# TensorE streams products of zeros between the small products of the landmark reading

## The chip, the cores and the metric

The kernel runs on one core of a Trainium2 chip. A core has TensorE (PE: products, its results go to the eight banks of PSUM), VectorE (DVE), ScalarE (ACT), GpSimd (POOL) and SyncE (SP), which here issues the DMAs. Each engine works through its own list of instructions in order and waits for the others on semaphores. The metric is the device time of one execution in microseconds (us), as the median of several runs; lower is better.

## The reference

A tower of one layer: a state-space tokenizer gives `h` of shape (16, 256, 512); an attention layer with landmarks and a feed-forward layer with block-wise quantized operands follow. The change lies in one step of the attention. There are 16 batch elements of 256 tokens, each cut in 4 blocks of 64 tokens (`S = 64`), with 4 landmarks per block (`M = 4`), 32 heads of 16 dimensions. After the landmarks have attended to one another, each reads the 64 tokens of its own block again:

```python
l2q = _split_heads(lmf @ w_l2t_q + b_l2t_q).reshape(B, H, Nb, M, DH)
ra = jax.nn.softmax(jnp.einsum('bhnmd,bhnsd->bhnms', l2q, kb) * scale, axis=-1)
ro = jnp.einsum('bhnms,bhnsd->bhnmd', ra, vb)
ro = ro.transpose(0, 2, 3, 1, 4).reshape(B, NL, D)
```

`kb` and `vb` are the rotated keys and the values of the tokens, computed in an earlier stage. All of it is float32.

## The kernel before

`build` runs seven stages, one after the other, each in its own `phase`: tokenizer, `attention_local`, `landmark_attention`, `landmarks_from_tokens`, `landmark_keys`, `attention_global`, `ffn`. At the end of a phase all engines meet at a barrier. Nothing of one stage runs beside another.

The change lies in `landmarks_from_tokens` alone. Its work is written out by hand for the 16 elements i, with two buffers of everything (`u = i % 2`). Per element:

- SP loads the keys `kT` and the values `v`, 512 KB each, from DRAM. The load of the keys of i waits until `scores(i-2)` is done, that of the values of i until `sums(i-2)` is done. SP issues in the order k(i), v(i), k(i+1), so the keys of i+1 also stand behind the wait of the values of i: they are issued right after `sums(i-2)`.
- DVE (`queries`) spreads the landmark queries over heads into `ql`.
- TensorE, `scores(i)` (L1490): 16 products, one for each block (Y = 4) and chunk of 128 channels (KC = 4), each with 32 stationary columns and 64 moving ones. The four chunks stand in four column groups of the array. A float32 product shows as two records in the profile, so there are 32.
- DVE, `maximum(i)` (L1441); ACT, `exp(i)` (L1405), 4 instructions with their sums; DVE, `norm(i)` (L1447, L1449).
- TensorE, `transposes(i)` (L1501): 2 transposes of 128x128.
- ACT, `copy(i)` (L1415): the transposed shares into `pT`.
- TensorE, `sums(i)` (L1513): 8 products with 128 stationary columns of `v` and 64 moving ones, 16 records.
- DVE, `pick(i)` (L1457, L1462): keeps each head's own part of the sums.

TensorE's order is: scores(0), and then for each i transposes(i), scores(i+1), sums(i). DVE's order is norm(i), queries(i+2), maximum(i+1), pick(i-1); ACT's is copy(i), exp(i+1). PSUM holds two banks each for scores, transposes and sums; two of its eight banks are unused in this stage.

Of the kernel before, what the change touches and what calls it, by code (L numbers as in the profile page):

```python
# [10 lines left out]
F32 = mybir.dt.float32  # L11
BF16 = mybir.dt.bfloat16
# [3 lines left out]
P = 128  # L16
# [1335 lines left out]
def landmarks_from_tokens(nc, K, k_s, v_s):  # L1352

    ctx = ExitStack()
    with ctx:
        def sb(name, shape, dt=F32):
            return ctx.enter_context(nc.sbuf_tensor("lt_" + name, shape, dt))

        def sem(name):
            return nc.alloc_semaphore("lt_" + name)  # L1360
# [4 lines left out]
        ql = sb("ql", [P, 2, KC, Y, 8 * M])  # L1365
# [1 line left out]
        pa = sb("pa", [P, 2, Y, S])  # L1367
        pT = sb("pT", [P, 2, 2, 2, P])
        lmx = sb("lmx", [P, KC * Y, M, 8])
        ps = ctx.enter_context(nc.psum_tensor("lt_ps", [P, 6, 512], F32))  # L1370
        scores_b = lambda u: ps[:, u]
        trans_b = lambda u: ps[:, 2 + u]
        sums_b = lambda u: ps[:, 4 + u]
        s_k, s_v = [[sem(f"{n}_in{u}") for u in range(2)] for n in ("k", "v")]
        s_zero, s_ql, s_sc, s_max, s_exp, s_rec, s_norm, s_tr, s_copy, s_sum, s_lmx, s_pick = (sem(n) for n in (
            "zero", "ql", "sc", "max", "exp", "rec", "norm", "tr", "copy", "sums", "lmxr", "pick"))
        block = ctx.enter_context(nc.Block())

        @block.sync
        def _(sp):  # L1380
            for i in range(BATCH):
                u = i % 2
                if i >= 2:
                    sp.wait_ge(s_sc, i - 1)
                sp.dma_start(kT[:, u].rearrange("p t c d -> p t (c d)"),
                             k_s[2 * i:2 * i + 2].rearrange("a p d -> p a d")).then_inc(s_k[u], 16)
                if i >= 2:
                    sp.wait_ge(s_sum, i - 1)
                sp.dma_start(v[:, u], v_s[2 * i:2 * i + 2].rearrange("a p d -> p a d")).then_inc(s_v[u], 16)

        @block.gpsimd
        def _(pool):
            pool.memset(pT[:], 0.0).then_inc(s_zero, 1)

        @block.scalar
# [83 lines left out]
        @block.tensor  # L1479
        def _(pe):  # L1480
            def scores(i):
                u = i % 2
                pe.wait_ge(s_k[u], 16 * (i // 2 + 1))
                pe.wait_ge(s_ql, i + 1)
                if i >= 2:
                    pe.wait_ge(s_exp, i - 1)
                for y in range(Y):
                    T, b = y // 2, y % 2
                    for k in range(KC):
                        ins = pe.matmul(scores_b(u)[32 * k:32 * k + 32, y * S:(y + 1) * S],  # L1490
                                        ql[:, u, k, y], kT[:, u, T, k, b * S:(b + 1) * S],
                                        start=True, stop=True)
                ins.then_inc(s_sc, 1)

            def transposes(i):
                u = i % 2
                pe.wait_ge(s_norm, i + 1)
                if i >= 2:
                    pe.wait_ge(s_copy, i - 1)
                for T in range(2):  # L1500
                    ins = pe.transpose(trans_b(u)[:, T * P:(T + 1) * P],  # L1501
                                       pa[:, u, 2 * T:2 * T + 2].rearrange("p b s -> p (b s)"), c("ident"))
                ins.then_inc(s_tr, 1)

            def sums(i):
                u = i % 2
                pe.wait_ge(s_v[u], 16 * (i // 2 + 1))
                pe.wait_ge(s_copy, i + 1)
                if i >= 2:
                    pe.wait_ge(s_lmx, i - 1)  # L1510
                for T in range(2):
                    for k in range(KC):
                        ins = pe.matmul(sums_b(u)[:, 128 * k + 64 * T:128 * k + 64 * T + 64],  # L1513
                                        v[:, u, T, k * P:(k + 1) * P], pT[:, u, T, :, 32 * k:32 * k + 32],
                                        start=True, stop=True)
                ins.then_inc(s_sum, 1)

            scores(0)
            for i in range(BATCH):
                transposes(i)  # L1520
                if i + 1 < BATCH:
                    scores(i + 1)
                sums(i)


# [686 lines left out]
class Kept:  # L2212
# [15 lines left out]
    def c(self, name):  # L2228
        a, b = CAT[name]
        return self.cst[:, a:b]  # L2230
# [24 lines left out]
def build(nc, A, consts_d, out):  # L2255
    def scratch(name, shape, dt=F32):
        return nc.dram_tensor(name, shape, dt, kind="Internal").ap()

    NT = 2 * BATCH
    h_s = scratch("h_s", (TOK, BATCH, D))  # L2260
    q_s, k_s, v_s = (scratch(n, (NT, P, D)) for n in ("q_s", "k_s", "v_s"))
    o_s = scratch("o_s", (NT, P, D + H))
    with ExitStack() as ctx:
        ctx.enter_context(nc.allow_non_contiguous_dma(reason="a few thousand scalars of parameters"))
        with phase(nc):
            tokenizer(nc, A, consts_d, h_s)
        K = Kept(nc, ctx)
        load_constants(nc, K, consts_d)
        with phase(nc):
            attention_local(nc, A, K, h_s, q_s, k_s, v_s, o_s)  # L2270
        with phase(nc):
            landmark_attention(nc, A, K, None)
        with phase(nc):
            landmarks_from_tokens(nc, K, k_s, v_s)
        gv_s = scratch("gv_s", (ROWS, D))
        with phase(nc):
            landmark_keys(nc, A, K, gv_s)
        h1_s = scratch("h1_s", (NT, P, D))
        with nc.sbuf_tensor("xqT", [P, KC, NT * P], BF16) as K.xqT:
            with phase(nc):  # L2280
                attention_global(nc, A, K, h_s, q_s, o_s, gv_s, h1_s)
            with phase(nc):
                ffn(nc, K, h1_s, out)
# [33 lines left out]
```

## Time and profile before

| | us |
|---|---|
| median of 3 runs | 1866.25 (1866.24 to 1870.73) |
| the profiled execution, its own time | 1858.75 |
| its span, first to last instruction | 1857.0 |
| PE busy | 1555.9 (84%) |
| DVE busy | 1378.5 (74%) |
| ACT busy | 986.5 (53%) |
| POOL busy | 495.0 (27%) |
| mean granted clock of TensorE | 0.872 |

The profile is one execution. A busy time of an engine is the union of its instructions' times. For TensorE that is no measure of how densely the array works: a product's record runs from its issue until its last result is out, so records of neighbours overlap, and small products that follow one another at twice their streaming time still make the engine 100% busy. PEclk is the clock that TensorE was granted, as a share of 2.4 GHz: 0.50 stands for 1.2 GHz. Mean durations of single records hold this tail; the distance from one product to the next is read from a run of equal ones: its length, less one record, over their number less one.

### The profile page before, as it was taken

What the parts mean: (1) busy time and instruction counts of PE and PEld (TensorE: products, weight loads), DVE (VectorE), ACT (ScalarE), POOL (GpSimd) and SP (SyncE); (2) the same over time, 40 slices, a digit from 0 to 9 for tenths busy, and PEclk for the clock granted to TensorE, in tenths of its full rate; (3) what the DMA queues carried; (4) which work ended last, traced back from release to release, by engine and by line L of the source; (5) the groups of instructions that cost most, each with busy time, mean ns of one, the idle gap of its engine ahead of it and who ended that gap; (6) DMA issues with size and microseconds to landing.
All of it is one profiled execution on the core that took longest, in us unless ns stands there. A gap on an engine that the chain in (4) does not pass through costs nothing. (4 is left out here: it accounts for less than half of the span.)

```text
span 1857.0 us, 35063 instructions
## 1 busy us (share of the span) xinstructions
PE 1555.9 (84%) x11938; PEld 1064.3 (57%) x12036; DVE 1378.5 (74%) x2642; ACT 986.5 (53%) x2531; POOL 495.0 (27%) x359
## 2 busy tenths in 40 slices
PE   2177749999999999999587896588888599999998
PEld 2177626667667677677366784455555244454444
DVE  8999936777777777777333461489988689999997
ACT  7566427787887887887421230455554233333332
POOL 0000014454444454444200000112212123333332
PEclk8555569999999999999886657799999799999999
DMA  2022251322222222222310452454443201111111
GB/s 57 12 46 57 57 158 66 114 74 84 87 85 87 101 74 97 75 85 97 111 39 1 166 198 81 126 155 126 136 149 104 72 23 45 51 45 45 45 45 51
DMA packets 122001, 154.54 MB, mean 83 GB/s; under 512 B 52562, under 2 KB 54226, under 8 KB 121939
## 3 DMA queue, kind: packets, MB, share of 16 engines
q1 hardware_dynamic: 121938, 153.76, 25.7%
q8 instruction: 34, 0.56, 0.1%
q14 instruction: 29, 0.23, 0.0%
HBM read 93.95 MB, written 59.77 MB: 83 GB/s over the span
## 5 line engine op out<-in xcount | busy, mean ns | idle before, releaser
L1048 PE MATMUL al_ps<-al_w,al_xT 128*128 128x512 f32 (+2 forms) x1024 | 351.3, 497 | 0.0
L1048 PEld LDWEIGHTS al_ps<-al_w,al_xT 128*128 128x128 f32 x1024 | 192.2, 193 | 127.1 <-issue 107.3
L2089 ACT ACTIVATE ff_zT<-ff_psz 128x1024 bf16<-128x1024 bf16 x64 | 65.5, 1024 | 237.6 <-PE ff_psz L2180 237.6
L433 PE MATMUL tk_ps<-tk_w,tk_l 128*128 128x64 f32 x512 | 113.0, 422 | 92.7 <-DVE tk_w L402 54.6
L2108 POOL TENSOR_TENSOR ff_zq<-ff_z,ff_back 128x1024 bf16<-128x1024 fp8e4 x64 | 122.2, 1909 | 250.8 <-DVE ff_z L2137 250.8
L433 PEld LDWEIGHTS tk_ps<-tk_w,tk_l 128*128 128x128 f32 x512 | 110.4, 332 | 95.3 <-issue 95.3
L730 POOL TENSOR_TENSOR al_qv<-al_qv,al_qe 128x512 f32<-128x512 f32 x48 | 61.9, 1289 | 248.5 <-PE al_ps L1121 248.5
L2163 PE MATMUL ff_gate<-wgT,xqT 128*128 128x512 bf16 x496 | 121.5, 383 | 3.8 <-ACTq L107 3.0
L2188 PE MATMUL ff_acc<-wdT,ff_zT 128*128 128x512 bf16 x512 | 122.6, 383 | 2.2 <-ACT ff_zT L2089 2.2
L2163 PE MATMUL ff_up<-wuT,xqT 128*128 128x512 bf16 x481 | 120.1, 381 | 1.6
L1949 PE MATMUL ag_ps<-ag_w,ag_aT 128*128 128x512 f32 x256 | 118.4, 605 | 0.0
L984 DVE TENSOR_REDUCE al_mx<-al_ps 128x32 f32<-128x2048 f32 x32 | 73.3, 2292 | 58.3 <-PE al_ps L1121 58.3
L876 ACT ACTIVATE al_p<-al_ps,al_mx 128x64 f32<-128x64 f32 x512 | 107.4, 354 | 0.0
L715 POOL TENSOR_TENSOR al_qk<-al_r 128x512 f32<-128x512 f32 x64 | 81.5, 1285 | 68.3 <-DVE al_r L924 68.3
L2163 PEld LDWEIGHTS ff_gate<-wgT,xqT 128*128 (+1 forms) x512 | 50.3, 98 | 64.0 <-ACTq L107 2.9
L2129 DVE TENSOR_TENSOR ff_z<-ff_sg,ff_up 128x1024 f32<-128x1024 f32 x64 | 77.8, 1216 | 11.9 <-PE ff_up L2163 10.0
L2188 PEld LDWEIGHTS ff_acc<-wdT,ff_zT 128*128 128x128 bf16 x512 | 50.3, 98 | 63.4 <-ACT ff_zT L2089 2.6
L1736 POOL TENSOR_TENSOR ag_xv<-ag_xn,ag_inv 128x1024 f32<-128x1024 f32 x16 | 30.6, 1911 | 206.7 <-DVEq L1903 206.7
L1746 POOL TENSOR_TENSOR ag_a<-ag_a,ag_o 128x1024 f32<-128x1024 f32 x16 | 37.6, 2349 | 170.5 <-DVE ag_a L1872 160.0
L1598 DVE TENSOR_REDUCE ff_eb<-ff_z 128x32 f32<-128x1024 f32 x64 | 78.1, 1220 | 4.8
L2134 DVE TENSOR_TENSOR ff_zv<-ff_z,ff_inv 128x1024 f32<-128x1024 f32 x64 | 78.4, 1224 | 2.2
L1949 PEld LDWEIGHTS ag_ps<-ag_w,ag_aT 128*128 128x128 f32 x256 | 46.0, 189 | 53.2 <-issue 53.2
(311 smaller groups left out, 3525.4 us busy)
## 6 DMA issues: line engine op xcount, KB each, us to landing
al_hx<-h_s SPq DMA_DIRECT2D x36, 256.0 KB, 2.8
o_s<-al_o SPq DMA_DIRECT2D x32, 272.0 KB, 2.1
h_s<-tk_w SPq DMA_DIRECT2D x16, 512.0 KB, 3.8
v_s<-al_v SPq DMA_DIRECT2D x32, 256.0 KB, 2.1
k_s<-al_kT SPq DMA_DIRECT2D x32, 256.0 KB, 2.4
q_s<-al_qT SPq DMA_DIRECT2D x32, 256.0 KB, 2.6
lt_kT<-k_s SPq DMA_DIRECT2D x16, 512.0 KB, 4.9
lt_v<-v_s SPq DMA_DIRECT2D x16, 512.0 KB, 3.7
```

The lines of the kernel that those rows point to most:

```text
L433: ins = pe.matmul(o, L[:, u, 0, t], R[:, u, t], start=True, stop=True)
L715: pool.tensor_tensor(qk[:, part * D:(part + 1) * D].rearrange("p (h d) -> p h d", d=DH), r1[:, heads], r2[:, heads], ALU.add).then_inc(out ...
L876: ins = act.activation(p[:, g, hd * S:(hd + 1) * S], ps[:, g, hd * S:(hd + 1) * S], ACT.Exp, bias=mx[:, 8 * g + hd:8 * g + hd + 1])
L984: dve.tensor_reduce(mx[:], ps[:, 0:4].rearrange("p b (h s) -> p (b h) s", s=S), AX.X, ALU.max, negate=True).then_inc(mx_r.sem, 1)
L1048: ins = pe.matmul(out, xT[:, T, k], w[:, k, cols], start=False, stop=True, skip_group_check=True)
L1598: st(eng.tensor_reduce(ebits.bitcast(F32), x, AX.X, ALU.max, apply_absolute_value=True))
L1949: ins = pe.matmul(out, aT[:, T, k], w[:, k], start=False, stop=(k == KC - 1))
L2108: pool.tensor_tensor(zq[:, u].rearrange("p (k s) -> p k s", s=QB), z8[:, u].rearrange("p (k s) -> p k s", s=QB), back[:, u, :, None].to_br ...
L2129: dve.tensor_tensor(z[:, u], sg[:, u], up[:].rearrange("p b n -> p (b n)"), ALU.mult).then_inc(z_r.sem, 1)
L2134: ls(dve.tensor_tensor(b3_(zv[:]), b3_(z[:, u]), inv[:, :, None].to_broadcast([P, NB, QB]), ALU.mult))
L2163: ins = pe.matmul(bank[:, n], K.xqT[:, k, bass.ds(t * P, P)], wT[:, k, (2 * hf + n) * D:(2 * hf + n + 1) * D], start=(k == 0), stop=(k == ...
L2188: ins = pe.matmul(acc[:, T], zT[:, u, k], K.wdT[:, 2 * KC * hf + k], start=(hf == 0 and k == 0), stop=(hf == 1 and k == 2 * KC - 1))
```

## The change

A tile `still` of zeros (128x512, bfloat16) is set by POOL ahead of its other memset, and a seventh PSUM bank is taken for results that nobody reads. `stream()` issues two products with the bfloat16 identity as stationary operand and the 512 columns of zeros as the moving one. TensorE waits for the zeros, streams 8 such products, and then, for each of the 16 elements, 2 after the transposes and 2 before the sums: 8 + 64 = 72 products.

```diff
+        still = sb("still", [P, 512], BF16)
-        ps = ctx.enter_context(nc.psum_tensor("lt_ps", [P, 6, 512], F32))
+        ps = ctx.enter_context(nc.psum_tensor("lt_ps", [P, 7, 512], F32))
...
         @block.gpsimd
         def _(pool):
+            pool.memset(still[:], 0.0).then_inc(s_still, 1)
             pool.memset(pT[:], 0.0).then_inc(s_zero, 1)
...
+            def stream():
+                for _ in range(2):
+                    pe.matmul(ps[:, 6], K.identb[:], still[:], start=True, stop=True)
+
+            pe.wait_ge(s_still, 1)
+            for _ in range(4):
+                stream()
             scores(0)
             for i in range(BATCH):
                 transposes(i)
+                stream()
                 if i + 1 < BATCH:
                     scores(i + 1)
+                stream()
                 sums(i)
```

TensorE at the start of the stage, before. The names are the PSUM tile and the two operands; L1347 is the last product of the stage ahead, L1490 scores, L1501 transposes, L1513 sums.

```order
L1347 MATMUL la_ps<-lmfT,la_wq 128x256 x16
L1169 UNCONDITIONAL_BRANCH
L1479 UNCONDITIONAL_BRANCH
L1490 MATMUL lt_ps<-lt_kT,lt_ql 32x64 x16
L1501 MATMUL lt_ps<-cst,lt_pa 128x128 x2
L1490 MATMUL lt_ps<-lt_kT,lt_ql 32x64 x16
L1513 MATMUL lt_ps<-lt_pT,lt_v 128x64 x8
```

The same place in the changed kernel, where lines below the new ones have other numbers: L1492 is scores, L1503 transposes, L1515 sums, and L1522 the streams.

```order
L1347 MATMUL la_ps<-lmfT,la_wq 128x256 x16
L1169 UNCONDITIONAL_BRANCH
L1481 UNCONDITIONAL_BRANCH
L1522 MATMUL lt_ps<-lt_still,identb 128x512 x8
L1492 MATMUL lt_ps<-lt_kT,lt_ql 32x64 x16
L1503 MATMUL lt_ps<-cst,lt_pa 128x128 x2
L1522 MATMUL lt_ps<-lt_still,identb 128x512 x2
L1492 MATMUL lt_ps<-lt_kT,lt_ql 32x64 x16
L1522 MATMUL lt_ps<-lt_still,identb 128x512 x2
L1515 MATMUL lt_ps<-lt_pT,lt_v 128x64 x8
```

Nothing of the old order moved; the streams stand between. The first pair of each element lies between its transposes and the next scores, the second between those scores and the sums.

## Rows read from the trace of the kernel before

**Rows 1.** Page: granted clock of TensorE in 40 slices of the span, tenths.

```profile
PEclk8555569999999999999886657799999799999999
```

**Rows 2.** Windows: stretch, its length, busy us (instructions) by engine, PEclk, DMA share, GB/s.

```profile
1080.00:1100.00 20.00, 19.53 (x199) 17.79 (x191) 12.76 (x24) 8.00 (x40) 0.00 (x0) 0.50 0.64 211
```

**Rows 3.** Timeline of one element: start, length, engine, line, operation, tiles, shapes.

```profile
1053.81 0.63 PE L1501 MATMUL lt_ps<-cst,lt_pa 128*128 128x128 f32 x2
1054.04 0.37 SPq L1389 DMA_DIRECT2D lt_v<-v_s  x1
1054.37 1.08 PE L1490 MATMUL lt_ps<-lt_kT,lt_ql 128*32 128x64 f32 x32
1054.46 0.47 SPq L1385 DMA_DIRECT2D lt_kT<-k_s  x1
1055.38 3.68 PE L1513 MATMUL lt_ps<-lt_pT,lt_v 128*128 128x64 f32 x16
1055.52 0.42 DVE L1441 TENSOR_REDUCE lt_nmax<-lt_ps 128x4 f32<-128x256 f32 x1 [1.78 <-PE lt_ps L1490]
1057.75 0.42 DVE L1449 TENSOR_TENSOR lt_pa<-lt_pa,lt_sum 128x256 f32<-128x256 f32 x1
1058.85 0.64 PE L1501 MATMUL lt_ps<-cst,lt_pa 128*128 128x128 f32 x2
1059.42 1.08 PE L1490 MATMUL lt_ps<-lt_kT,lt_ql 128*32 128x64 f32 x32
```

**Rows 4.** Timeline at the stage's start and end.

```profile
1030.69 0.95 POOL L1393 MEMSET lt_pT<- 128x1024 f32 x1 [126.55 <-POOLq L2252]
1034.93 1.08 PE L1490 MATMUL lt_ps<-lt_kT,lt_ql 128*32 128x64 f32 x32 [5.59 <-DMA lt_kT<-k_s]
1038.13 0.42 DVE L1449 TENSOR_TENSOR lt_pa<-lt_pa,lt_sum 128x256 f32<-128x256 f32 x1
1038.61 0.69 PE L1501 MATMUL lt_ps<-cst,lt_pa 128*128 128x128 f32 x2 [2.61 <-DVE lt_pa L1449]
1039.23 1.08 PE L1490 MATMUL lt_ps<-lt_kT,lt_ql 128*32 128x64 f32 x32
1110.62 1.08 PE L1490 MATMUL lt_ps<-lt_kT,lt_ql 128*32 128x64 f32 x32
1116.64 3.65 PE L1513 MATMUL lt_ps<-lt_pT,lt_v 128*128 128x64 f32 x16 [0.90 <-issue]
```

**Rows 5.** Landing of the 16 loads of keys (L1385), and who waited for them.

```profile
  PEld lt_ps L1490: 9.4, 9
DMA to landing us min/median/max: 4.2/4.9/5.5
```

**Rows 6.** Timeline: PE in local attention, feed-forward and landmark attention.

```profile
891.55 1.00 PE L513 MATMUL al_ps<-ap_pT,al_v 128*128 128x64 f32 x8
896.03 0.43 PE L1103 MATMUL al_ps<-al_kT,al_pqs 128*32 128x128 f32 x8 [0.25 <-ACT al_kT L839]
1605.12 1.89 PE L2188 MATMUL ff_acc<-wdT,ff_zT 128*128 128x512 bf16 x8
1012.44 9.14 PE L1341 MATMUL la_ps<-la_loT,la_wo 128*128 128x256 f32 x32 [0.69 <-ACT la_loT L1225]
```

**Rows 7.** Windows of 3 and 4 us, columns as in rows 2.

```profile
893.00:897.00 4.00, 3.21 (x78) 2.66 (x74) 2.43 (x11) 2.02 (x4) 0.00 (x0) 1.00 0.02 4
958.00:961.00 3.00, 1.87 (x13) 1.34 (x14) 2.79 (x5) 2.56 (x5) 0.00 (x0) 1.00 0.00 0
1013.00:1016.00 3.00, 3.00 (x8) 2.36 (x7) 0.00 (x0) 0.00 (x0) 0.00 (x0) 0.50 0.00 0
1016.00:1020.00 4.00, 4.00 (x19) 3.48 (x18) 1.07 (x3) 0.00 (x0) 0.00 (x0) 0.94 0.01 4
1028.00:1032.00 4.00, 1.33 (x7) 0.83 (x5) 1.89 (x4) 0.00 (x0) 0.95 (x1) 1.00 0.02 7
1032.00:1036.00 4.00, 1.07 (x32) 0.84 (x32) 0.02 (x1) 0.00 (x0) 0.00 (x0) 0.69 0.99 338
```

More of the change, by code:

```diff
@@ L1374, in landmarks_from_tokens @@
         s_k, s_v = [[sem(f"{n}_in{u}") for u in range(2)] for n in ("k", "v")]
-        s_zero, s_ql, s_sc, s_max, s_exp, s_rec, s_norm, s_tr, s_copy, s_sum, s_lmx, s_pick = (sem(n) for n in (
-            "zero", "ql", "sc", "max", "exp", "rec", "norm", "tr", "copy", "sums", "lmxr", "pick"))
+        s_zero, s_ql, s_sc, s_max, s_exp, s_rec, s_norm, s_tr, s_copy, s_sum, s_lmx, s_pick, s_still = (sem(n) for n in (
+            "zero", "ql", "sc", "max", "exp", "rec", "norm", "tr", "copy", "sums", "lmxr", "pick", "still"))
         block = ctx.enter_context(nc.Block())
```

## The prediction

> **What bounds the kernel now.** I read the page first: TensorE is the busiest engine of the table, and its clock is below full in the tokenizer's slices and again between slices 19 and 26 [rows 1]. Counted from 0, slices 22 to 24 hold the stage that is changed. The windows over it come second [rows 2]: PE is busy 19.53 us of 20, at a granted clock of 0.50, that is 1.2 GHz, and the slices beside it say the same for nearly all of a stage of some 90 us. So here TensorE works without a pause and still at half clock.
>
> The timeline of one element is third [rows 3]. Scores start at 1054.37 and again at 1059.42: a period of 5.05 us. On TensorE it is made of transposes 0.56 (1053.81 to 1054.37), scores 1.01 (to 1055.38) and sums 3.47 (to 1058.85), in all 5.04. TensorE's stream is one bound.
>
> Two others lie close under it. The first is the loop through softmax: scores start 1054.37, maximum starts 1.15 later, the normalized shares are done at 1058.17 (1057.75 + 0.42), 2.65 after the maximum's start, and the next transposes could start some 0.05 later (0.06 at the first element, 1038.55 to 1038.61 [rows 4]). With 0.56 for the transposes that is 1.15 + 2.65 + 0.05 + 0.56 = 4.4 us. The second is the loop of the keys' load. The values' DMA is issued when a block of sums ends (1054.04), the keys' 0.42 later, and these land 4.9 us after their issue, 5.5 at the most [rows 5]: 1054.46 + 4.9 = 1059.36, and the scores that need them start at 1059.42. Nine waits of the weight loads for keys are booked [rows 5]. Taken from the scores one period ahead of 1054.37, through their sums (end 1054.04) and the load to 1059.42, it is 10.1 us for two elements, so this loop too stands at 5.05 per element. Whoever speeds up TensorE must look at that one next.
>
> **The price of the two clocks.** I take the distance between equal products. At half clock the 16 records of sums take 3.68 us with a tail of about 0.42: 3.26/15 = 0.217 us each [rows 3]. The same shape in local attention at full clock: 8 in 1.00 with a tail of 0.275, so 0.104 [rows 6], and the window behind it grants 1.00 [rows 7]. Eight 512-column bfloat16 products take 1.89 us at full clock, 0.38 of it tail: 0.215 each [rows 6]; at half clock I take twice that, 0.43. The scores at half clock come in fours, one four per 0.11 ((1.08 - 0.31)/7) [rows 3]. At full clock the nearest row is the same form with 128 columns instead of 64: two fours in 0.43, 0.13 apart [rows 6]. So a four of 64 columns costs between 0.055 (half of 0.11) and 0.13; I take 0.07, which makes a block of scores 0.55 to 0.6 us instead of 1.01 (bounds 0.5 and 1.1).
>
> **Does the clock rise?** The rows show it rising after dense work: the 256-column products of L1341 start at 1012.44, PE is busy 3.00 of 3 at 0.50 until 1016, and 0.94 is the mean of the next 4 us [rows 6, 7]. It falls after little work: 1.33 and then 1.07 us busy of 4 and the clock is lost within 1032 to 1036 [rows 7]. In between it keeps what it has. Full clock was kept over 958 to 961 with only 1.87 of 3 us busy, and over the 64-column and 34-column products of 893 to 897 [rows 7]; half clock was kept over this whole stage, whose sums leave the array half unused (a 64-column float32 product every 0.217 us). The added products change the cold mix. Transposes, stream, scores, stream become about 3.3 us of dense work in one piece at half clock, then sums 3.47. That piece looks like the stretch ahead of the rise at 1016, so I expect the clock to rise in the first or second element. Once full, TensorE's stream is 3.6 us of a period of 4.4 (below), with a pause under 1 us, which is no thinner than the stretches that kept full clock. So it stays.
>
> The Trainium skill, "TensorE: Matmul & The Clock Gate", section "What's actually happening", says that the throttle follows how busy the engine has recently been. The trace agrees only in part: 19.53 of 20 us busy and 0.50 granted, so the busy column is not that measure. Read by the column alone, the change could raise nothing and would only cost its streams.
>
> **The sum, part by part.**
>
> Memset of zeros, ahead of the other on POOL: the larger one takes 0.95 from 1030.69 [rows 4]. TensorE waits for it until at most 1031.7, and ACT's wait for the other moves by as much; ACT has nothing to do before 1036. Free. The 8 first products take 1.7 (full clock, which was still granted until about 1033 [rows 7]) to 3.4 us (half) and end at 1033 to 1035.1. Keys land just ahead of 1034.93 [rows 4], so 0 to 0.2; I take 0. What hides them is that first load.
>
> New period at full clock. TensorE: transposes 0.35, stream 0.43, scores 0.6, stream 0.43, sums 16 x 0.104 to 0.112 = 1.75: 3.6 us. Softmax loop: 0.85 from scores to maximum (1.15 less what the scores gain), 2.65 + 0.05 unchanged, transposes 0.35, and the first stream 0.43, which lies on this loop: 4.33. Loop of the keys: scores start to end of sums is 0.6 + 0.43 + 1.75 + a tail and switches 0.3 = 3.1, then 0.06 + 0.42 + 4.9 + 0.1: 8.6 for two elements, 4.3 each. The second stream lies on this loop and not on the other. The two are equal to within what I can read, and late loads will push now one, now the other: I take 4.4. Lower bound 4.2 (keys at 4.7), upper 4.65 (keys always at 5.5).
>
> First interval, scores(0) to scores(1): the first stream at half clock, + 0.86. The 14 intervals from 1039.23 to 1110.62 take 71.39 now [rows 4]. Two of them I set at 5.6, the mean of 4.4 and the all-cold 6.76 (5.04 + 4 x 0.43), twelve at 4.4: 64.0, a gain of 7.4. The end: from scores(15) at 1110.62 to 1120.29 (1116.64 + 3.65) is 9.67 [rows 4]. After: 0.85 + 2.7 to the last transposes, then 0.35 + 0.86 + 1.75 + 0.16 = 3.1: 6.7, a gain of 3.0. Sum: -7.4 - 3.0 + 0.9 = -9.5 us.
>
> Later stages start 9.5 us earlier and do the same work. Their clock changes at instants that the program doesn't set, which may cost or give 1 us. The profiled execution would go from 1858.75 to 1849.25. Its own time is 7.5 below the median of the runs shown; taking the difference over, 1866.25 - 9.5 = 1856.75.
>
> **The rivals.**
>
> (a) The clock stays at half, because zeros through an identity do not wake it, or because half-used sums stand in every stretch. The period is then TensorE's cold stream, 6.76 us: 14 x 1.71 = 23.9, + 0.86 at the start, + 2.6 at the end (0.86 for the stream ahead of sums(14), 1.71 for the last element), 27.4 in all: 1893.6. For it: half clock over 90 us of full busyness [rows 2]. Against it: the rise at 1016, and the array is then used well over what it is now. No row shows products of zeros. It decides as soon as the clock is at half for more than about a quarter of the stage, since a cold period loses 1.71 and a warm one gains 0.65.
>
> (b) The clock goes up and down by turns: the pause of 0.8 us before the transposes and the thin sums lose what the streams won. Half of the intervals at 6.76 and half at 4.4 make 5.6 on the mean: 14 x 0.55 = 7.7, + 0.9, - 0.6 at the end: +8, 1874. For it: the landmark attention ahead of this stage has a mean clock of 0.6 to 0.8 in some slices [rows 1], and loses it within 1032 to 1036 after work of 1.33 us in 4 [rows 7]. Against it: there the pauses are longer, and 958 to 961 kept its clock.
> The Trainium skill, same page, section "A second HAM failure mode: psum-queue depth-cycling", tells of a kernel that cycled PSUM banks and whose clock went up and down because of short idles between groups. No row here shows it at pauses as short as these.
>
> (c) The clock rises, but the keys come late: with less time between loads they land at 5.5, the worst value now, and the period is 4.65: the gain is 3.0 + 71.39 - (11.2 + 55.8) - 0.9 = 6.5, so 1859.8. For it: 211 GB/s now, and 240 or more then. Against it: 338 GB/s in the first load [rows 7]. At a landing of 6.4 nothing but the end would be left, 1864.
>
> **How the numbers follow.** Forecast 0.60 (its own range 1853 to 1860), (a) 0.10, (b) 0.10, (c) 0.20. A difference of under 0.3%, 5.6 us, is what a measurement of this kernel can't tell from none. Faster: 0.57 of the forecast and 0.12 of (c), 0.69. Same: 0.03 + 0.08 + 0.02 of a mild (b), 0.13. Slower: 0.18. The range reaches from 1851 (period 4.1 and an early rise) to 1867, and leaves out (a), most of (b) and little below.
>
> **What would show it.** Right: PEclk 1.00 in the windows from about 1050 on, sums of 16 in about 1.9 us instead of 3.68, periods of 4.3 to 4.5 between scores, TensorE idle before transposes (released by L1449's successor) or before scores (released by the keys). Wrong in the clock: 0.50 in those windows, periods of 6.8. Wrong in the loops: full clock and periods over 4.7, with the waits of scores for keys growing beyond 9.4 us.

## The result, and the profile after

The changed kernel takes 1854.54 us (median of 6 runs, 1850.52 to 1859.07), the kernel before on the same chip 1868.2 (6 runs, 1866.24 to 1871.23). The ratio is 0.9928, 95% interval 0.9908 to 0.9948: 13.4 us less, between 9.7 and 17.2. I had forecast 1856.8, which was 9.5 us under the 1866.25 of the runs shown. The profiled execution has a span of 1850.9 us (1857.0 before).

Page of the changed kernel, granted clock in 40 slices:

```profile
PEclk8555569999999999999786898799999799999999
```

Against [rows 1], slice 22 has gone from 6 to 8 and slice 23 from 5 to 9. Windows of the changed kernel over the stage (columns as in [rows 2]: stretch, length, busy us and instructions of PE, PEld, DVE, ACT, POOL, then PEclk, DMA share, GB/s):

```profile
1034.00:1038.00 4.00, 1.67 (x7) 0.69 (x8) 1.32 (x3) 0.00 (x0) 1.41 (x2) 1.00 0.49 156
1038.00:1042.00 4.00, 0.65 (x32) 0.49 (x32) 0.80 (x3) 1.29 (x8) 0.00 (x0) 0.88 1.03 387
1042.00:1046.00 4.00, 3.38 (x40) 2.29 (x41) 1.25 (x3) 1.39 (x7) 0.00 (x0) 0.50 0.31 117
1046.00:1050.00 4.00, 4.00 (x19) 3.42 (x18) 1.21 (x3) 1.07 (x7) 0.00 (x0) 0.50 0.00 0
1050.00:1054.00 4.00, 3.51 (x50) 2.90 (x50) 2.46 (x5) 1.64 (x9) 0.00 (x0) 0.84 0.79 264
1062.00:1082.00 20.00, 16.65 (x257) 13.41 (x261) 14.82 (x30) 9.40 (x45) 0.00 (x0) 1.00 0.72 239
```

The clock is still full at the first scores, falls near 1041 in the pause ahead of the first transposes, is back near 1051 in the second element, and stays at 1.00 until the last sums (the 0.85 of 1102 to 1122, not shown, has the end of the stage in it; the last sums still take 1.97). PE's busy share has fallen from 19.53 to 16.65 us of 20, with more instructions in it: the engine is no longer the bound. Timeline of one element of the changed kernel, which answers to [rows 3] (rows between these are left out, and of the second pair of streams the trace has one record only):

```profile
1066.88 0.44 PE L1503 MATMUL lt_ps<-cst,lt_pa 128*128 128x128 f32 x2 [0.51 <-DVE lt_pa L1451]
1067.16 0.59 PE L1522 MATMUL lt_ps<-lt_still,identb 128*128 128x512 bf16 x2
1067.68 0.65 PE L1492 MATMUL lt_ps<-lt_kT,lt_ql 128*32 128x64 f32 x32
1068.40 0.42 DVE L1443 TENSOR_REDUCE lt_nmax<-lt_ps 128x4 f32<-128x256 f32 x1 [0.97 <-PE lt_ps L1492]
1068.49 0.38 PE L1522 MATMUL lt_ps<-lt_still,identb 128*128 128x512 bf16 x1 [0.16 <-issue]
1068.71 1.89 PE L1515 MATMUL lt_ps<-lt_pT,lt_v 128*128 128x64 f32 x16
1070.64 0.42 DVE L1451 TENSOR_TENSOR lt_pa<-lt_pa,lt_sum 128x256 f32<-128x256 f32 x1
1071.05 1.28 SPq L1386 DMA_DIRECT2D lt_kT<-k_s  x1
1071.12 0.44 PE L1503 MATMUL lt_ps<-cst,lt_pa 128*128 128x128 f32 x2 [0.51 <-DVE lt_pa L1451]
1071.91 0.65 PE L1492 MATMUL lt_ps<-lt_kT,lt_ql 128*32 128x64 f32 x32
```

The period is 4.23 us (1067.68 to 1071.91). Sums have gone from 3.68 to 1.89, scores from 1.08 to 0.65. The bracket says what PE waits for now: the normalized shares. Along that loop, scores to maximum takes 0.72, maximum to the end of norm 2.66 (1071.06), then 0.06, and from the transposes to the next scores 0.80, of which a good half is the stream. That is 4.24, the whole period. Who waited for whom in this stage, changed kernel (total us, times, longest):

```profile
PE lt_ps L1503 <- DVE lt_pa L1451: 9.8, 15, 2.6
PEld lt_ps L1492 <- DMA lt_kT<-k_s: 6.5, 9, 2.2
PE lt_ps L1492 <- DMA lt_kT<-k_s: 2.5, 3, 1.7
PEld lt_ps L1522 <- POOL lt_still L1394: 2.3, 1, 2.3
```

Of the fifteen waits of the transposes for DVE one, 2.6 us at the first element, was there before; fourteen are new. Those for keys are still there; two of them lengthen a period, to 4.56 and 4.87.

**Where the time went.** From the first scores to the end of the last sums the stage took 85.36 us and takes 74.49 (1039.02 to 1113.51): 10.9 less. The span fell by only 6.1, since the stages ahead of this one took 4.2 us longer in this execution. There the two programs do the same. Windows over the same stretch at the end of local attention, with the same 93 TensorE records in each, the first of the kernel before, the second of the changed one:

```profile
904.50:911.70 7.20, 6.63 (x93) 6.07 (x93) 1.12 (x3) 6.32 (x24) 0.00 (x0) 0.81 0.00 0
```

```profile
905.70:915.90 10.20, 9.72 (x93) 8.95 (x93) 1.09 (x3) 6.46 (x24) 0.00 (x0) 0.50 0.00 0
```

Granted clock 0.81 in one execution and 0.50 in the other, for the same instructions: 3.0 of the 4.2 us. So the clock does not change at the same instruction in every execution. Times differ from run to run by more than that: 29 later runs of the kernel before lie between 1861.23 and 1872.61, and how much of this spread is clock was not isolated. The profiled execution of before, 1858.75, is below every one of its timed runs. A stage's own length is the sharper measure here, and below both are given; "stage" always means first scores to end of last sums in the profile.

### The profile page after: what moved, and what is told of

It is laid out like the page before. It is cut to its first block and busy times, and to the rows that moved or that the text cites. A ratio compares the mean times of both kernels' runs of the same rounds, so it can differ in the third digit from the quotient of the medians.

```text
span 1850.9 us, 35192 instructions
## 1 busy us (share of the span) xinstructions
PE 1540.9 (83%) x11994; PEld 1044.8 (56%) x12108; DVE 1378.1 (74%) x2642; ACT 987.2 (53%) x2531; POOL 495.9 (27%) x360
```

## The experiments

Each is compared with the kernel before on the same chip, and is an edit of the changed kernel. A stage's length and its periods come from one profiled execution each, the time and the ratio from all timed runs. A period is the distance between the starts of two blocks of scores.

### Is one push at the start enough?

```diff
                 transposes(i)
-                stream()
                 if i + 1 < BATCH:
                     scores(i + 1)
-                stream()
                 sums(i)
```

> Only the 8 products of zeros ahead of scores(0) stay; the 64 between the elements are left out. Theory (the streams between the elements hold the clock): the 8 products keep or raise it for a moment, it falls in the pause before the first transposes, and from then on the stage runs at 0.50 with periods of 5.05 us; time as the kernel before within 0.3% (ratio 0.997 to 1.003). Rival (the clock keeps whatever it has once raised, and one push at the start is enough): PEclk 1.00 over the stage, periods near 4.0, ratio to before 0.993 or less.

Measured: ratio 0.9995 (0.998 to 1.001), stage 86.78 us; the first period is 4.26, as in the kernel before (4.30), and the others are 5.04 to 5.86.

```profile
1040.00:1044.00 4.00, 1.08 (x34) 0.78 (x34) 1.51 (x4) 1.29 (x8) 0.00 (x0) 0.81 1.02 347
1048.00:1068.00 20.00, 18.67 (x194) 16.53 (x193) 10.95 (x22) 7.08 (x33) 0.00 (x0) 0.50 0.54 179
```

The clock is lost in the first pause and does not come back in this stage. The tile, the bank, the memset and the first 8 products do nothing for the time by themselves; the gain is made by the 64 products between the elements.

### Does the clock hold once it is up?

Streams at the start and in elements 0 to 2 only:

```diff
-                stream()
+                if i < 3:
+                    stream()
```

(at both places)

> The streams stay at the start and in elements 0 to 2, and are left out for elements 3 to 15. Theory (once the clock is full, the small products and pauses under 1 us keep it): PEclk 1.00 to the end of the stage, softmax loop 3.80 us, keys loop (0.6 + 1.8 + 0.2 + 0.06 + 0.42 + 4.8 + 0.1) / 2 = 4.0, period 4.0 to 4.1: 12 x 0.2 = 2.4 us under the changed kernel, ratio to before 0.991. Rival (the streams must go on to hold it): the clock falls back to 0.50 some elements after the third and the period returns to 5.05: ratio 0.998 to 1.002.

Measured: ratio 0.9993 (0.9979 to 1.0007), stage 85.94. The rival came out. After those of elements 0 and 1, the periods are 4.57, 3.84, 4.18, 4.93, 4.84, and from then on 5.04 or more. Timeline of PE where it falls:

```profile
1067.32 1.98 PE L1515 MATMUL lt_ps<-lt_pT,lt_v 128*128 128x64 f32 x16
1070.15 0.44 PE L1503 MATMUL lt_ps<-cst,lt_pa 128*128 128x128 f32 x2 [0.85 <-DVE lt_pa L1451]
1071.64 0.88 PE L1492 MATMUL lt_ps<-lt_kT,lt_ql 128*32 128x64 f32 x32 [1.06 <-DMA lt_kT<-k_s]
1072.45 3.68 PE L1515 MATMUL lt_ps<-lt_pT,lt_v 128*128 128x64 f32 x16
```

The clock falls right after two pauses, the second for keys; the slowest load of keys in this profile landed 5.7 us after its issue. So either the thin work or the late load could be the cause. The next run parts them.

### Was it the late load?

The same with SP's list in another order, so that keys no longer stand behind values:

```diff
+            keys(0)
+            values(0)
+            keys(1)
+            values(1)
+            keys(2)
+            for i in range(2, BATCH):
+                if i + 1 < BATCH:
+                    keys(i + 1)
+                values(i)
```

(`keys(i)` and `values(i)` hold the old waits and DMAs)

> Streams only at the start and in elements 0 to 2, as before, and SP's list in the order that issues the keys of i+1 early. Theory X (the fall in element 6 of the run with the first three was brought by the late keys, 5.72 us, which left TensorE idle): with no late keys the clock stays 1.00, periods 3.80 to the end, stage (first scores to end of last sums) about 69 us. Theory Y (the small products alone, with the pause of about 0.9 us in a period of 3.8, are too thin to hold it): the clock falls to 0.50 a few elements after the third although no load is late, periods return to 5.05, stage about 84 us.

One run, no interval: 1858.55 us, stage 77.26. Seven periods of 3.80 follow on the third, and then come one of 4.98 and four of 5.05:

```profile
1075.00:1081.00 6.00, 4.87 (x93) 4.13 (x93) 4.84 (x9) 3.61 (x18) 0.00 (x0) 1.00 0.93 307
1081.00:1085.00 4.00, 3.46 (x49) 2.94 (x49) 3.14 (x7) 2.00 (x11) 0.00 (x0) 0.76 0.87 274
1085.00:1095.00 10.00, 10.00 (x102) 9.00 (x101) 6.18 (x13) 3.90 (x20) 0.00 (x0) 0.50 0.66 208
```

TensorE waited for no load there. Theory Y: without the streams this stage keeps full clock for a while, but not for good. Without streams the sums of elements 3 to 8 still ran at full clock here, and those of 3 and 4 in the run before. That the late load made the difference fits, but it is one profile each. Note the busy column: 4.87 of 6 at full clock, 10.00 of 10 at half.

### Are both places needed?

Only the products ahead of the sums:

```diff
                 transposes(i)
-                stream()
                 if i + 1 < BATCH:
                     scores(i + 1)
                 stream()
```

> The 8 at the start and the 2 before each sums stay, the 2 after the transposes go, so nothing is added on the softmax loop. Theory A (the piece of dense work must be long: transposes, stream, scores, stream): with half of it gone the clock stays 0.50 or rises late; at 0.50 the period is 5.05 + 0.86 = 5.9 and the time 13 us over the kernel before, ratio 1.007. Theory B (a little more streaming is enough): PEclk 1.00, period set by softmax loop 0.72 + 2.66 + 0.05 + 0.37 = 3.80 or keys loop about 4.1, so 4.1, and 1 to 2 us under the changed kernel, ratio to before 0.992.

Measured: ratio 0.9963 (0.9948 to 0.9978), a median of 1858.87 us, and a stage of 84.37 in a profiled execution that took 1865.25, so most executions probably had a shorter one. Neither theory: the clock goes up and down.

```profile
1053.00:1060.00 7.00, 6.03 (x71) 5.01 (x70) 5.88 (x11) 3.38 (x19) 0.00 (x0) 0.96 0.77 268
1060.00:1064.00 4.00, 3.67 (x44) 3.14 (x45) 2.51 (x6) 1.99 (x10) 0.00 (x0) 0.57 0.77 262
1064.00:1070.00 6.00, 4.49 (x66) 3.62 (x69) 3.88 (x8) 2.81 (x12) 0.00 (x0) 1.00 0.62 203
1070.00:1077.00 7.00, 7.00 (x87) 5.73 (x88) 3.89 (x8) 2.29 (x12) 0.00 (x0) 0.55 0.45 159
```

This is the picture of my rival (b). The swing resembles what the Trainium skill describes in "TensorE: Matmul & The Clock Gate", section "A second HAM failure mode: psum-queue depth-cycling"; the trace agrees with the swing alone (0.96, 0.57, 1.00 and 0.55 in stretches of one stage). The section puts the short idles down to cycling through PSUM banks. Here the clock falls in the first pause, as in the other kernels, and four times more, near 1060, 1071, 1095 and 1115, and just ahead of each of the four stands a wait for keys: 0.42, 0.98, 1.21 and 2.14 us. Who waited for keys over the stage, and the third of these falls:

```profile
PE lt_ps L1492 <- DMA lt_kT<-k_s: 9.1, 10, 2.1
```

```profile
1093.38 0.65 PE L1492 MATMUL lt_ps<-lt_kT,lt_ql 128*32 128x64 f32 x32 [1.21 <-DMA lt_kT<-k_s]
1094.41 3.38 PE L1515 MATMUL lt_ps<-lt_pT,lt_v 128*128 128x64 f32 x16
```

The changed kernel has 2.5 us in 3 such waits. This edit was not run with early keys, so half the dose and late keys are not parted here.

### Which loop sets 4.23 us?

The changed kernel with the order of SP's list shown above.

> The changed kernel, with SP's list written in another order: the keys of i+1 are issued ahead of the wait for sums(i-2), so they no longer stand behind the values of i. Theory (the softmax loop with the first stream on it sets the period of 4.23 us): the period stays 4.23 and only the two late loads (0.33 and 0.64 us) go: 1.0 us under the changed kernel, within noise. Rival (the keys loop sets it): the period falls towards TensorE's 3.7 us, 6 us under the changed kernel, ratio to before 0.990.

Measured: ratio 0.9928 (0.9909 to 0.9946), stage 73.42 us. From the fourth on, every period is 4.23 or 4.24, and the only wait of the scores for keys is that for the first load:

```profile
PE lt_ps L1505 <- DMA lt_kT<-k_s: 1.7, 1, 1.7
```

So the softmax loop sets it, and the keys loop costs only when a load is late: 1.07 us in the changed kernel's profile, as foreseen.

### Do the values that are streamed matter?

```diff
-            pool.memset(still[:], 0.0).then_inc(s_still, 1)
+            pool.memset(still[:], 1.0).then_inc(s_still, 1)
```

> The tile that is streamed holds ones instead of zeros; nothing else differs from the changed kernel. Theory (the clock follows what is streamed, not its values): stage 74.5 us, periods 4.23, time within 0.2% of the changed kernel, ratio to before 0.993. Rival (values count): the clock is up earlier or held by fewer products; visible as an earlier first window of 1.00 than in element 2.

Measured: ratio 0.9959 (0.9943 to 0.9975), stage 77.54, PEclk back to full in the same place (the sums of element 0 take 3.51 us and those of element 1 1.89, with zeros 3.51 and 1.90), and a mean clock of 0.93 over the stage as with zeros. The clock behaves as the theory says; the time misses my number. The 3.1 us by which the stage is longer are periods of 4.41 to 5.68 in which scores wait for keys, whose worst landing was 6.5 us:

```profile
PE lt_ps L1492 <- DMA lt_kT<-k_s: 5.4, 5, 1.7
```

Against 2.5 us in 3 waits with zeros. The keys' DMA neither reads nor writes the tile. That late keys are a matter of chip and moment is likely, since the next two kernels show them too, but it is argued and not tested: the kernel with zeros was not run beside this one. The ratios differ by 5.8 us, more than the stage explains.

### The start of the stage

Without the first 8 products:

> The changed kernel without the 8 products ahead of scores(0). Theory (the clock is lost in the pause before the first transposes with them as without, and won back by elements 0 and 1): stage 74 to 75 us, time as the changed kernel within 0.2%. Rival (they shorten the way to full clock): the first window of 1.00 comes an element later, 2 us slower.

Measured: ratio 0.9949 (0.9931 to 0.9968), stage 77.99. With 10 more products after scores(0):

```diff
             scores(0)
+            for _ in range(5):
+                stream()
             for i in range(BATCH):
```

> The changed kernel with 10 more products right after scores(0). Theory (elements 0 to 2 of the changed kernel pay 0.5 + 2.3 + 0.4 us over 4.23 for the clock lost in that pause): clock 1.00 from the first scores, stage 71.3 us, 3.2 us under the changed kernel in the stage and in the time, ratio to before 0.991. Rival (the later stages give it back by where their half-clock stretches fall): stage 71.3 and time as the changed kernel, ratio 0.993.

Measured: ratio 0.9966 (0.9954 to 0.9979), stage 76.06. The second one does hold the clock: 1.00 from the start, and the first periods are 4.07, 4.00 and 4.23 instead of 4.74, 6.57 and 4.66. But both profiles have late keys (four periods between 4.67 and 5.55 without the first 8, three of 5.05 to 5.50 with the 10 more), and in both the clock was lost once more behind them. PE of the kernel with 10 more:

```profile
1091.00 0.38 PE L1522 MATMUL lt_ps<-lt_still,identb 128*128 128x512 bf16 x1
1092.57 1.08 PE L1492 MATMUL lt_ps<-lt_kT,lt_ql 128*32 128x64 f32 x32 [1.19 <-DMA lt_kT<-k_s]
1093.59 1.03 PE L1522 MATMUL lt_ps<-lt_still,identb 128*128 128x512 bf16 x2
1094.42 3.51 PE L1515 MATMUL lt_ps<-lt_pT,lt_v 128*128 128x64 f32 x16
```

A wait of 1.19 us for keys, and scores and sums at half-clock prices behind it: the next period was 6.57. So a late load costs its own length and may cost the clock for an element. My number for this run, 71.3, left that out. What the first 8 products are worth these two don't settle. Without them scores(0) ran at half clock (1.08 us), yet the clock was back in element 0, an element earlier than in the changed kernel and not later as the rival had it; the stage missed the 74 to 75 us of the theory by its late keys.

The kernel with 10 more gains less time than the changed kernel: the intervals, 0.9954 to 0.9979 and 0.9908 to 0.9948, don't meet. Its profile is 4.9 us longer (1855.8 against 1850.9), of which the stage makes 1.6, global attention 1.0 and the feed-forward stage with what follows 2.8 (377.3 against 374.5). That last part takes either 374.5 to 374.9 or 377.3 to 377.8 us in all the profiles, whatever the edit; why was not looked into.

### The streams in the pause, and early keys

The pair after the transposes moved behind the sums, where PE waits for norm anyway, and the early keys:

```diff
                 transposes(i)
-                stream()
                 if i + 1 < BATCH:
                     scores(i + 1)
                 stream()
                 sums(i)
+                if i + 1 < BATCH:
+                    stream()
```

> The two products after the transposes are moved behind the sums, into TensorE's pause ahead of the next transposes; SP's list issues the keys early. Theory (softmax loop binds and the first stream lies on it): the period falls from 4.23 by 0.43 to 3.80 to 3.9 at full clock, 12 x 0.4 = 5 us under the run with early keys, ratio to before 0.990. Rival (the clock needs the dense piece of transposes, stream, scores, stream): it drops to 0.50 in part of the windows and the time is that of the changed kernel or above, ratio 0.993 to 1.0.

Measured: ratio 0.9895 (0.9878 to 0.9912), 1845.17 us, stage 67.05, every period after the third 3.80 or 3.81. Timeline of this kernel (L1535 are the streams):

```profile
1076.07 0.59 PE L1535 MATMUL lt_ps<-lt_still,identb 128*128 128x512 bf16 x2
1076.13 0.42 DVE L1464 TENSOR_TENSOR lt_pa<-lt_pa,lt_sum 128x256 f32<-128x256 f32 x1
1076.61 0.44 PE L1516 MATMUL lt_ps<-cst,lt_pa 128*128 128x128 f32 x2
1076.98 0.65 PE L1505 MATMUL lt_ps<-lt_kT,lt_ql 128*32 128x64 f32 x32
```

The products end at about the moment the shares are ready, and from the transposes to the scores it is 0.37 instead of 0.80. The same number of products between elements, less two, holds the clock, and 0.43 us per element come off the loop. Against the run with early keys, which differs only by the place of the streams, the stage is 6.4 us shorter. With its second run below (0.9882, interval up to 0.9901) this kernel beats both the one before and the changed one.

With the 10 products after scores(0) as well:

> As fill, with 10 more products right after scores(0), in the pause of 2.6 us in which TensorE waits for the first normalized shares. Theory (the clock falls there for want of work, and elements 0 to 2 pay for it with 4.74, 6.57 and 4.66 us): PEclk 1.00 from the first scores to the last sums, all periods near 3.85, 3 us under fill, ratio to before 0.988. Rival (clock lost there anyway, or the 10 products delay the first transposes by up to 1.7 us): no gain over fill.

Measured: ratio 0.9894 (0.9876 to 0.9912), 1846.55 us, stage 63.37 with PEclk 1.00 all through: 3.7 us less stage, and no less time. Both were run once more, side by side:

> The kernel of the run fill once more, beside the next one on the same chip: stage 67 us, time about 1845.5.

> The kernel of the run fill_hold once more. The stage is 3.7 us shorter than that of fill. Theory (its profiled execution met an unlucky place of the half-clock stretches in global attention, 323.6 us against 318.5, which varies from run to run): 3.7 us under fill_b, about 1842. Rival (it starts the later stages at an instant from which they always lose it): equal to fill_b again.

Measured: 1843.65 us and 0.9882 (0.9862 to 0.9901) without the 10 products, 1843.79 and 0.9883 (0.9863 to 0.9903) with them; stages 67.26 and 63.99. The rival, as far as the times can tell: the medians agree, but by the scatter of the runs a difference of some 4 us stays open in each pair and of some 3 in both together, so the times alone only just exclude the gain. The profiles show where it went: global attention, up to the first instruction of the feed-forward stage, takes 318.5 and 320.0 us in the two profiles without and 323.6 and 323.4 in the two with. The 20 us that begin some 16 us into it, without (first fence) and with the 10 products:

```profile
1163.00:1183.00 20.00, 11.96 (x63) 11.18 (x65) 11.39 (x15) 10.45 (x29) 2.35 (x1) 0.74 0.26 75
```

```profile
1160.00:1180.00 20.00, 11.47 (x63) 10.48 (x63) 11.89 (x15) 9.89 (x28) 2.35 (x1) 0.67 0.24 73
```

The same work at a mean clock of 0.74 and 0.67; in the other pair it is 0.74 and 0.67 again. I read this part as thinly filled stretches that miss or catch the full clock by the instant at which they start; no run isolates that. Another part is not of the clock. TensorE's first product of global attention waits for a small load, `ag_b`, and from the stage's first DMA issue to the first product with keys it is 13.3 to 13.4 us in the three profiles of kernels with the 10 more products, and 11.6 to 12.2 in the eleven others. That is 1.5 of the 5.1 us in the first pair and 1.1 of the 3.4 in the second, and as far as fourteen profiles can tell it goes with the program and not with the moment. Waits for that load in fill (first) and in fill_hold:

```profile
PE ag_ps L2005 <- DMA ag_b<-ag_b_parts: 15.0, 1, 15.0
```

```profile
PE ag_ps L2007 <- DMA ag_b<-ag_b_parts: 16.5, 1, 16.5
```

Why the load comes later, and why the clock is the worse one in both profiles, stays open.

## Why the prediction was right

The forecast's mechanism is what happened, and the measured time lies in its own range. The forecast difference, 9.5 us, is just below the interval of the measured one, and the difference is the sharper test. By its steps:

- **The clock rises and stays.** Right for this kernel: back in the second element, 1.00 to the end. Wrong in the reason that it would keep it. "No thinner than the stretches that kept full clock. So it stays" would hold for the stage without streams as well, and there, early keys or not, the clock was lost again [first_three, first_three_keys]. The busy columns that I compared don't carry that argument. What kept the clock is that the streams went on, and the argument did not use them.
- **The prices.** Sums 1.75 plus tail expected, 1.89 measured; scores 0.55 to 0.6 expected, 0.65; two products of zeros 0.43 apart from their tail, and 0.52 from L1522 to L1492.
- **The period.** Taken as 4.4, is 4.23. The softmax loop had been put at 4.33: scores to maximum is 0.72 and not 0.85. The keys loop, put at 4.3, is just under it: early keys save 1.07 us and change no other period. So rival (c) is real and small here; in the runs with ones, without the start and with the 10 more it costs more.
- **The sum.** Scores 1 to 15: 63.01 us (1043.75 to 1106.76) against 64.0 expected and 71.39 before; the first two of these intervals, 6.57 + 4.66 = 11.23, met the 11.2 put down for them, while each was set at 5.6. First interval 0.43 longer than before, not 0.86, since the clock was still full at scores(0). The end 6.75 (1106.76 to 1113.51) against 6.7. In all -8.4 + 0.4 - 2.9 = -10.9 where I had -9.5.
- **The time.** 13.4 us, interval 9.7 to 17.2. The stage explains 10.9. The kernel with early keys, which differs from the changed one by about 1 us, took 12.1 us less than 29 runs of before (1866.44), so the rest of the 13.4 may be scatter or the changing place of half-clock stretches in other stages, which cost 3.0 us in the one profile. That share was not isolated, and the sum does not contain it: that the time came within 2.3 us of the forecast, although the difference was 3.9 off, is in part luck: the median of before from which the forecast started lies 2 us below that of the later six runs.
- **Rival (a)** is out: 1.00 with zeros, and the same with ones.
- **The memset** takes 0.53 us of its own, TensorE waited 2.3 us for it from its last work on, and the keys landed 1.7 us after the 8 products had ended: free, as said.

## What to carry to other kernels

Where TensorE is busy for a whole stage and its granted clock stays at 0.50, as under the small products here, products that nobody reads can buy the other clock: here 1.7 us of them at half clock turned a period of 5.05 into 4.23. Put them into pauses of the engine and not on the chain that other engines wait for (3.80), keep them up for the whole stage, and take away late loads first, since each may cost the clock too. Measure the stage and the whole apart: 3 to 4 us gained in one stage did not show in the time, and a later one was longer in both profiles.

## What I had not expected of the hardware

- Half the dose gave neither clock for good: with 2 products per element it swung between 0.55 and 1.00, and the stage of the profile, at 84.37 us, gained only 1.0. The time fell by 0.37%, half of what the full dose brought. Late keys had a part in it that was not isolated.
- One granted clock for a stage hides when it was lost: a mean of 0.93 over the stage of the kernel with 10 more products contains a whole element at half clock, 6.57 us instead of 4.23, set off by a wait of 1.19.
- The load of 512 KB of keys landed after 4.2 to 7.4 us within one stage (the run with streams ahead of the sums only), with 4.2 to 5.5 in the profile before.
